# Second cross attention: values and probabilities in high and low parts, value products over two head pairs, ScalarE's work reordered within a pair

## The reference, cut to what matters

```
xn   = layernorm(ctx_1024) * ln1_w + ln1_b     # 16 x 1601 x 128
latn = layernorm(x) ...                        # 16 x 64 x 128
kv_input = concatenate([xn, latn], axis=1)     # 1665 keys
k, v = split(kv_input @ Wkv);  q = latn @ Wq   # 16 heads of 64
weight = softmax(q k^T / sqrt(64));  out = (weight @ v) @ Wo
x = x + out
```

## Time and the profile before

| | us |
|---|---|
| median of 3 runs | 1934.91 (1932.0 to 1936.72) |
| profiled execution, its own time | 1935.08 |
| its span, first to last instruction | 1933.3 |
| second cross attention, first scores to last output | 787.5 to 1792.95 |
| mean granted TensorE clock over the span | 0.945 of full speed |

### The profile page before, as it was taken

The page is one execution under the profiler, slowest core; times in us unless marked ns, Lnnn a source line. Parts: engine busy times, 40 slices in busy tenths (PEclk is TensorE's granted clock), DMA queues, the critical chain, the costliest instruction groups (busy, mean ns, idle before and its releaser), DMA issues. The chain is left out here.

```text
span 1933.3 us, 33380 instructions
## 1 busy us (share of the span) xinstructions
PE 1710.4 (88%) x11692; PEld 1210.4 (63%) x11692; DVE 1233.6 (64%) x3059; ACT 857.0 (44%) x1939; POOL 526.8 (27%) x708
## 2 busy tenths in 40 slices
PE   6998999999988993599999999999999999999423
PEld 3665666666667883466766666666666676665322
DVE  7666666666655774666666656666666666653577
ACT  2555555555552441344444444444444444442222
POOL 2000000000012222324553245423543345411223
PEclk8999999999998997799999999999999999999665
DMA  5533535353400112100000000000000000000000
GB/s 145 133 86 88 134 97 120 86 120 86 103 2 1 45 66 107 46 23 23 29 29 12 17 28 28 11 28 17 28 28 11 18 28 28 1 1 1 1 5 5
DMA packets 32659, 90.35 MB, mean 47 GB/s; under 512 B 8552, under 2 KB 17424, under 8 KB 32528
## 3 DMA queue, kind: packets, MB, share of 16 engines
q1 hardware_dynamic: 32384, 88.09, 16.9%
q10 hardware_dynamic: 144, 0.61, 0.2%
HBM read 40.43 MB, written 8.91 MB: 26 GB/s over the span
## 5 line engine op out<-in xcount | busy, mean ns | idle before, releaser
L2221 PE MATMUL c_pv_ps<-c_prob_t,c_xn 128*128 128x512 f32 (+2 forms) x896 | 413.4, 598 | 0.0
L340 ACT ACTIVATE c_prob<-c_score_ps,c_neg_max 128x512 f32<-128x512 f32 (+1 forms) x512 | 304.8, 608 | 64.3 <-PE c_scratch L2207 35.0
L986 DVE TENSOR_REDUCE a_chunk_max<-a_side_ps 128x1 f32<-128x512 f32 (+1 forms) x416 | 261.0, 665 | 112.2 <-PE a_side_ps L737 111.9
L359 DVE TENSOR_REDUCE c_chunk_max<-c_score_ps 128x1 f32<-128x512 f32 (+1 forms) x512 | 291.2, 581 | 48.6 <-PE c_score_ps L266 47.1
L237 PE MATMUL c_turn_ps<-consts,c_prob 128*128 128x128 f32 (+2 forms) x1792 | 286.4, 277 | 11.9 <-DVE c_prob_t L369 11.2
L237 PEld LDWEIGHTS c_turn_ps<-consts,c_prob 128*128 128x128 f32 (+2 forms) x1792 | 212.6, 140 | 97.2 <-issue 32.4
L2221 PEld LDWEIGHTS c_pv_ps<-c_prob_t,c_xn 128*128 128x128 f32 (+2 forms) x896 | 158.4, 191 | 164.6 <-issue 164.5
L373 DVE COPY c_prob_t<-c_turn_ps 65x128 f32<-65x128 f32 (+1 forms) x256 | 61.4, 279 | 298.6 <-PE c_turn_ps L237 298.6
L894 ACT ACTIVATE a_prob<-a_st_ps 128x1024 f32<-128x1024 f32 (+1 forms) x224 | 214.5, 958 | 53.9 <-PE a_st_ps L721 53.9
L266 PE MATMUL c_score_ps<-c_x_hi,c_q_hi 128*128 128x512 f32 (+1 forms) x512 | 218.6, 427 | 2.7 <-ACT c_prob L340 1.9
L324 ACT ACTIVATE c_prob_t<-c_turn_ps 128x512 f32<-128x512 f32 x128 | 76.4, 597 | 276.1 <-PE c_turn_ps L237 274.4
(11 more groups left out here) (318 smaller groups left out, 2595.5 us busy)
## 6 DMA issues: line engine op xcount, KB each, us to landing
a_stack<-a_k_hi SPq DMA_DIRECT2D x126, 200.1 KB, 4.1
a_stack<-a_k_lo SPq DMA_DIRECT2D x63, 200.1 KB, 4.2
a_ctx<-in_ctx_dram SPq DMA_DIRECT2D x16, 768.0 KB
c_ctx<-in_ctx_dram SPq DMA_DIRECT2D x16, 768.0 KB
absorbed_queries<-b_q_out SPq DMA_DIRECT2D x16, 512.0 KB, 3.4
c_q_raw<-absorbed_queries SPq DMA_DIRECT2D x16, 512.0 KB, 3.3
w<-in_L_ffn_w_dram SPq DMA_DIRECT2D x2, 512.0 KB
fold_raw<-in_L_xattn_Wkv_dram SPq DMA_DIRECT2D x2, 512.0 KB
```

What stands on the lines that cost most here:

```text
L340: nc.scalar.activation(prob[s % 2][:, cols], score_ps[:, cols], ACT.Exp, bias=neg_max[:, s % 2:s % 2 + 1], accum_out=sums[:, (s // QUAD) % ...
L359: nc.vector.reduce_max(chunk_max[:, s % 2, c:c + 1], score_ps[:, quad_chunk(c, keys)], AX_X).then_inc(chunk_max_done, 1)
L986: nc.vector.reduce_max(out, rows, AX_X).then_inc(side_taken, 1)
L2221: last = nc.tensor.matmul(lay.own.pv_ps[:], t.xn[m][0:rows, i, :], lay.own.prob_t[u][0:rows, i, :], start=(i == 0), stop=(i == LAT))
```

## The change

Only the second cross attention changes.

- Value product: instead of one f32 matmul for each key tile and quad (512 columns), three fp32r matmuls for each key tile and "duo" of two pairs (256 columns): low rows by high probabilities, high by high, high by low. `prob_t` is replaced by `p_hi` and `p_lo`; `xn` becomes one buffer, and new buffers `v_hi` and `v_lo` (two each) hold the split rows. `weigh_values` does 7 key tiles in each slot, in two parts for each duo, and begins three slots behind a duo's first pair instead of five behind a quad's.
- ScalarE writes the high parts of all four turned chunks (`high_halves`); VectorE writes the low parts as a difference of the turned bank and the high part (`low_halves`), which takes the place of its copies.
- Scores "in twos": TensorE waits once for two chunks, does chunks 0 and 1, turns chunks 0 and 1 of the pair before, then does chunks 2 and 3, the value product, the job at "a", and turns chunks 2 and 3. The exponentials are two (1024 and 641 columns), the maxima three (1024, 512 and 129).
- ScalarE's order in a slot: high parts 0 and 1, job "b", the two exponentials, high parts 2 and 3, job "a". VectorE's: low parts 2 and 3 of the pair two before, maxima, low parts 0 and 1, job "b", statistics.
- GpSimd gets `split_rows` for each batch, behind `make_diag` of the batch's first quad. The jobs `norm` and `out` stand two slots earlier.

```diff
-    half = [None] * 7 + [("norm",), None, xt[0], xt[1], None, xt[2], None, xt[3], ("norm",)]
-    lay.jobs = [half[:11] + [("out",)] + half[12:], half]
+    half = [None] * 3 + [("norm",)] + [None] * 5 + [xt[0], xt[1], ("norm",), xt[2], None, xt[3], None]
+    lay.jobs = [half[:7] + [("out",)] + half[8:], half]
...
         def pe_values(pe, m, u, tiles):
             for i in tiles:
-                if i < len(lay.tiles):
-                    rows = lay.tiles[i][0]
-                    last = nc.tensor.matmul(lay.own.pv_ps[:], t.xn[m][0:rows, i, :], lay.own.prob_t[u][0:rows, i, :],
-                                            start=(i == 0), stop=(i == LAT))
+                rows = lay.tiles[i][0]
+                out, v_hi, v_lo = lay.own.pv_ps[:, DUO * P * u:DUO * P * u + DUO * P], t.v_hi[m][0:rows, i, :], t.v_lo[m][0:rows, i, :]
+                nc.tensor.matmul(out, v_lo, lay.own.p_hi[u][0:rows, i, :], start=(i == 0), stop=False)
+                nc.tensor.matmul(out, v_hi, lay.own.p_hi[u][0:rows, i, :], start=False, stop=False)
+                last = nc.tensor.matmul(out, v_hi, lay.own.p_lo[u][0:rows, i, :], start=False, stop=(i == LAT))
...
# TensorE, turn: every turning waits for the low part of the chunk two before
-            if c == 0 and not first:
-                pe.wait_ge(copied_act, pair)
-            if c == 1 and not first:
-                pe.wait_ge(copied_dve, 3 * pair)
-            if c >= 2:
-                pe.wait_ge(copied_dve, 3 * pair + c - 1)
+            if c >= 2 or not first:
+                pe.wait_ge(low_done, CHUNKS * pair + c - 1)
...
# TensorE, body
-                    if before:
-                        pe.wait_ge(exp_done, (pair - 1) * CHUNKS + c + 1)
+                    if before and c % 2 == 0:
+                        pe.wait_ge(exp_done, (pair - 1) * 2 + c // 2 + 1)
...
-                    if before and c != 2:
-                        turn(k, kind, s, min(c, 2))
+                    if before and c == 1:
+                        turn(k, kind, s, 0)
+                        turn(k, kind, s, 1)
...
-                i, part = (s // QUAD - 1, s % QUAD - 1) if s % QUAD else (s // QUAD - 2, CHUNKS - 1)
+                i, part = ((s - 3) // 2, 0) if s % 2 else ((s - 4) // 2, 1)
...
                 if before:
-                    turn(k, kind, s, CHUNKS - 1)
+                    turn(k, kind, s, 2)
+                    turn(k, kind, s, 3)
...
# ScalarE, body
+                if before:
+                    high_halves(k, kind, s, 0)
+                    high_halves(k, kind, s, 1)
                 at(k, kind, s, "b")
-                if not (kind == "first" and s == 0):
-                    copy_turned(k, kind, s)
...
-                for c in range(CHUNKS):
-                    cols = quad_chunk(c, keys)
+                for c, cols in enumerate(exps_of):
                     nc.scalar.activation(prob[s % 2][:, cols], score_ps[:, cols], ACT.Exp, bias=neg_max[:, s % 2:s % 2 + 1],
                                          accum_out=sums[:, (s // QUAD) % 2, j, c:c + 1]).then_inc(exp_done, 1)
-                    if c == 1:
-                        at(k, kind, s, "a")
+                if before:
+                    high_halves(k, kind, s, 2)
+                    high_halves(k, kind, s, 3)
+                at(k, kind, s, "a")
...
# VectorE, low_halves
+            dve.wait_ge(high_done, pair * CHUNKS + c + 1)
+                last = nc.vector.tensor_tensor(p_lo[u][part], turn_ps[c % 2][:].rearrange("p (t q) -> p t q", t=4), p_hi[u][part].bitcast(F32), ALU.subtract)
...
# GpSimd
+        def split_rows(eng, ops, b, m, first, waits):
+            if not first:
+                wait_apart(eng, lay.own.pv_done, CHUNKS * QUADS * (b - 1), waits)
+            wait_apart(eng, t.xn_done, CHUNKS * (b + 1), waits)
+            for c in range(CHUNKS):
+                for rows, tiles in (((P, slice(4 * c, 4 * c + 4)),) if c < 3 else ((TAIL, slice(FULL, FULL + 1)), (SEQ, slice(LAT, LAT + 1)))):
+                    last = ops.tensor_copy(t.v_hi[m][0:rows, tiles, :], t.xn[0:rows, tiles, :])
+                last.then_inc(t.v_high, 1)
+            for c in range(CHUNKS):
+                eng.wait_ge(t.v_high, CHUNKS * b + c + 1)
+                (the same tiles: v_lo = xn - v_hi, then_inc(t.v_split, 1))
```

More of the change, by code:

```diff
@@ L39 @@
 SLOTS = 2 * PAIRS
+DUO = 2
+DUOS = SLOTS // DUO
 LN_EPS = 1e-5
@@ L92, in number_jobs @@
                 finishes = job is not None and job[0] in ("norm", "out")
-                if job is None or (kind == "first" and finishes and s < 7) or (kind == "last" and m == 1 and not finishes):
+                if job is None or (kind == "first" and finishes and s < 5) or (kind == "last" and m == 1 and not finishes):
                     continue
@@ L210, in _ @@
         body(BODIES - 1, "last")
-        make_diag(2 * BATCH - 1, own.number_after(BODIES - 1, "last", 15, "a"))
+        make_diag(2 * BATCH - 1, own.number_after(BODIES - 1, "last", 13, "a"))
     @block.tensor
@@ L240, in weigh_values @@
         def weigh_values(k, i, part):
-            q = 4 * k + i
-            m, u = quad_of(i)
+            e, q = DUOS * k + i, 4 * k + i // 2
+            m, u = quad_of(i // 2)
             if part == 0:
-                pe.wait_ge(copied_dve, (q + 1) * QUAD * 3)
-                pe.wait_ge(copied_act, (q + 1) * QUAD)
-                if not (isinstance(q, int) and q == 0):
+                pe.wait_ge(low_done, (e + 1) * DUO * CHUNKS)
+                if i % 2 == 0 and not (isinstance(q, int) and q == 0):
                     pe.wait_ge(pv_taken, q)
-            last = lay.pe_values(pe, m, u, range(4 * part, min(4 * part + 4, len(tiles))))
+                if i % 4 == 0:
+                    lay.pe_values_ready(pe, 2 * k + i // 4)
+            last = lay.pe_values(pe, m, i % 2, range(7 * part, 7 * part + 7))
             last.then_inc(pv_done, 1)
@@ L288, in _ @@
         body(BODIES - 1, "last")
+        pe.wait_ge(exp_done, BATCH * PAIRS * 2)
         for c in range(CHUNKS):
-            pe.wait_ge(exp_done, (BATCH * PAIRS - 1) * CHUNKS + c + 1)
             turn(BODIES, "mid", 0, c)
[L293 to L296, removed]
+        weigh_values(BODIES, -2, 1)
+        weigh_values(BODIES, -1, 0)
+        job(("norm",), base("last", BODIES - 1) + len(table["last"]), 0, "mid", BODIES, 1)
+        weigh_values(BODIES, -1, 1)
         if lay.last_output:
-            job(("out",), base("last", BODIES - 1) + len(table["last"]) + 1, 0, "mid", BODIES, 5)
+            job(("out",), base("last", BODIES - 1) + len(table["last"]) + 1, 0, "mid", BODIES, 3)
     @block.scalar
@@ L416, in body @@
-                if s % QUAD == 1 and not (kind == "first" and s < QUAD):
+                for c in range(CHUNKS - 1):
+                    lay.dve_between(dve, k, kind, s, c)
+                if s % QUAD == 0 and not (kind == "first" and s < QUAD):
                     denominators(4 * k + s // QUAD - 1, (s // QUAD - 1) % 2)
-                if s % QUAD == 0 and not (kind == "first" and s < 2 * QUAD):
-                    finish_quad(k, s // QUAD - 2, own.number_after(k, kind, s - 1, "a"))
+                if s % QUAD == 2 and not (kind == "first" and s < QUAD + 2):
+                    finish_quad(k, s // QUAD - 1, own.number_after(k, kind, s - 1, "a"))
```

131 lines of the change are left out of this document (76 added, 55 removed).

## The result

The changed kernel takes 1907.99 us (median of four runs, 1905.13 to 1909.08) where the kernel before takes 1934.71 (1932.0 to 1936.72): a ratio of 0.986, with a 95% interval of 0.9845 to 0.9875. It is faster by 27 us. The forecast was 77, and 1908 lies above the range of 1832 to 1900. The profiled execution's own time is 1909.08, its span 1907.3; the mean granted clock of TensorE is 0.943, as before.

The account below looks back on a forecast made before the run. The prediction took TensorE's own instruction stream to set the stage's time. From 1935.1 us it took 60 for the value product and 17 for waits, giving 1858 us, with a range of 1832 to 1900.

Parts of the forecast that it names:

- The value product: TensorE: 84 fp32r matmuls a quad at 0.121 us take 10.2 us against 12.0, in all -60 us.
- The first rival: Value product on TensorE: weight loads stop hiding, at least 0.24 us a matmul, +261, about 2180 us; 5%.
- ScalarE, VectorE: Work per slot: ScalarE 4.1 us, hidden beside TensorE's 6.46; VectorE 4.8, 6.9 in slot 2, so slot 3 waits 0.5.
- The ring: Chain through ScalarE and VectorE in a slot: 5.8 us, below TensorE's 6.46, so it does not set the pace.
- GpSimd: Diagonal for `norm`: TensorE waits 1.0 us in the second batch of a body, none in the first.
- Start and tail: Ends of the stage: waits in slots 0 to 5 fall from 17 to 12 us; the tail takes 22.5 instead of 34.
- Waits after: TensorE's waits in the middle slots: 3.0 us a body at most, some 20 us in 7.5 bodies, against 28.
- hand-over of `x_t`: Chunks 0 and 1 at the end of slot 4 and early in slot 5: costs 0.5 us in each batch.
- the schedule: Whole stage: all waits 35 us instead of 52, -17 us.
- Rival 5: The gain goes elsewhere and nothing is left, for instance at the loop's edges; 2%.
- Rival 2: Value product's pace: the full 0.1375 us a matmul, about 1903, 8%; or the floor 0.11, 1830, 7%.
- rivals 3 and 4: Second cross attention: VectorE or ScalarE becomes the bound, 1898 us, 10%; GpSimd is late, 1884 us, 9%.

Follow-up runs that it names:

- e3: Changed kernel with only one pass of three (high rows by high probabilities) in the value product, low parts still made: 1847.53 us.
- e7: Changed kernel with full 128 rows, middle bodies written out on three engines, and GpSimd making a batch's first diagonal between chunks of its normalised rows: 1851.77 us.
- e9: Changed kernel with one f32 matmul of 256 columns per key tile and duo in place of the three fp32r passes: 1955.03 us.
- e1: Changed kernel with TensorE's loop over the six middle bodies written out: 1886.61 us.
- e4: Changed kernel with the middle bodies written out on TensorE, VectorE and ScalarE: 1877.58 us.

## Why the prediction was wrong

The mechanism of the gain was right. The sum was not: it had a cost of the change at nothing, and took another for a wait that would go. By its steps:

- **The value product, -60.** Right. The pace is 0.117 us against 0.121 taken. A quad took 12.33 us before and takes 10.44 now (12.0 and 10.2 were the forecast's), in both cases with the steps at the short tiles: 32 times -1.89 is -60. The first rival is refuted. The Trainium skill says (TensorE: Matmul & The Clock Gate, "The mechanism") that a weight load overlaps a running matmul only when the row groups differ, though the opening of the same section also has loads into a background weight buffer pulled ahead; in this trace 0.117 us a matmul holds a weight load of its own, between matmuls on the same 128 rows. The extra time stands where the number of rows changes.
- **ScalarE, VectorE.** Mostly right. Their busy shares of the middle are 57% and 72% (60 and 70 forecast). The exponential of 1024 columns took 1.12, a difference 0.69, the high parts 0.60 and 0.37. VectorE's 1024 column maximum took 1.22. The wait at the head of slots 3 and 11 costs 0.8 from start to start and not 0.5: +4.5 us. That was a slip of addition: the prediction's own terms for slot 2 (4.8, five statistics of 0.28, 0.5 and 0.67) make 7.4 and not 7.0; the trace has 7.6 from one low part to the next (1160.46 to 1168.05).
- **The ring.** 5.8 forecast; e3 shows 6.2 to 6.3. It was too short for want of hand-overs, and still hidden.
- **GpSimd.** Right in place: the wait for the diagonal is in slot 13 (8.79) and not in slot 5. Its size is 0.6 instead of 1.0 while TensorE is slowed elsewhere; e7 shows that it costs 10 us once TensorE is not.
- **Start and tail.** The start 43.15 (the prediction's terms make 43.4: 26.4 and 5 of work, 12 of waits), the tail 24.3 (22.5).
- **Waits after, "some 20 us" in the middle.** This is the step that failed. I counted the engines' waits for each other, and those are there: 8.4 + 5.4 + 4.0 = 17.8 us in three of the four rows of waits. I took what was left of the 28 us before as waits of the same kind that would go. They were partly something else. Some 10 us (32 quads at 0.3) were the steps at the short tiles, which I had priced at the even pace. The new product meets them 64 times and not 32, with slots of 6.74 beside ones of 6.38: +20 to 23 us against the forecast. And the 448 more loads and matmuls of a body came in the sum as time on the engine and never as something to be fetched: five edges at a mean of 3.1 us in slot 15 and 1.5 in slot 0, +23.

The list adds up. Edges +23, short tiles +22, heads of slots 3 and 11 +4.5, hand-over of `x_t` in slots 7, 15 and 5 some +8, start and tail +2, and the pace of 0.117 with the first steps in it -12: 47 to 48 of the 50 us by which the stage missed. The +22 and the -12 belong together, which is why the product's own step came out right. e9 splits the same 50 another way: the schedule was forecast at -17 and gave +20, the passes at -60 and gave -47. These two make 50 by their definition, so they are no second proof of the list.

The experiments weigh the two big items by their removal. Writing out the loops gives 30 us, of which 14 were there before. Full rows give 11 alone and 16 after the loops (1877.6 to 1861.5). With both gone the kernel takes 1861.5, 3.5 from the forecast. That is no proof of the forecast, since 14 us of this are a gain that the kernel before could have had too.

Rival 5 named "the loop's edges" and had 2%, without a place or price. In the earlier trace rows the edge of the old body cannot be seen, since TensorE's costs nothing there; the trace of before shows a limit only on its far side. The other engines' edge could be seen: slot 0 takes 7.6 to 7.9 us behind each of the five edges of that trace, and 5.99 elsewhere. So could the queue of instructions, at 0 packets in the loop, with a body that was to grow by more than a third.

Rival 2 (a pace of 0.1375 or 0.11) is out by the pace, rivals 3 and 4 by the waits above. Of the theories behind the runs, C is no cause as the kernel stands, and D is half true. ScalarE's job at the end is worth its 30 us against the job in the middle, but the schedule as a whole, measured alone, costs 20. The order of scores and turnings was never undone by itself, so its own share is not shown.

**Still open.** At which size of body TensorE's edge starts to cost: 1192 loads and matmuls are free, 1416 (e9) are too, 1640 are not. What fills the gap: the packet that starts with it takes 0.95 us of its 2.6. In e1 the queue still moves 106 packets, 27 of them between 1030 and 1513, and TensorE stands still for none of them; so it is not the fetching that costs but the jump back to what has to be fetched. And e9's 20 us are only in part assigned.

## What to carry to other kernels

When a change multiplies the instructions in a loop body, count them and look at the instruction queue of the profile: price the edge of the loop at a few us for each pass (here 2.8 idle in the mean, and mostly the lower clock in the slot behind), or write the loop out. Read a pace across all neighbours, also where the shape changes: 0.3 us at a short tile hides in "waits" until the tile is met twice as often. Of an in-order engine's jobs, put the one whose input comes late behind those on which others wait: one line was worth 30 us.

## What the runs showed of the hardware

- A loop edge is free for TensorE with a body of 1192 or 1416 weight loads and matmuls, and costs 2.6 to 3.1 us of idle time with 1640, where a 16 KB packet of the instruction queue starts in each of the five gaps. Behind four of them the clock falls to one half (0.80 over the slot at 1267.32); behind the one at 1146.19 it doesn't. Written out, the same code brings its packets without a gap (e1). VectorE stands still for 2.5 to 2.8 us at its edge in either kernel; with the loops written out 1.6 to 1.7 are left in the changed kernel (e4), which are a wait for ScalarE.
- Between matmuls of 64 rows and matmuls of 65 or 128, two steps of 0.20 to 0.23 us stand in place of 0.117; zeroed rows up to 128 remove them.
- A fp32r matmul of 256 columns with a weight load of its own starts every 0.117 us; in e3, where only a third of them is left, plain slots stop at 6.2 us, with TensorE waiting for VectorE's low parts.
